# Scores of one head per bank and a fourth bank for row maxima, in two attention stages of one kernel

## The reference, cut to what matters

```python
att = jnp.einsum('bsgmd,btgd->bgmst', q, k) / scale
causal = jnp.triu(jnp.ones((s, s), bool), 1)
att = jnp.where(causal, -jnp.inf, att)
att = jax.nn.softmax(att, axis=-1)
ctx = jnp.einsum('bgmst,btgd->bsgmd', att, v).reshape(b, s, DIM)
```

## Time and profile before

| what | value |
|---|---|
| median of 3 runs | 5195.83 us (5181.3 to 5202.37) |
| profiled execution | 5158.03 us |
| its span | 5156.5 us |
| mean granted clock of TensorE | 0.887 |
| attention B, first to last score | 198.7 to 1006.6 us |
| attention G, first to last score | 2316.2 to 3166.8 us |

### The profile page before, as it was taken

The page is one execution under the profiler, slowest core; times in us unless marked ns, Lnnn a source line. Parts: engine busy times, 40 slices in busy tenths (PEclk is TensorE's granted clock), DMA queues, the critical chain, the costliest instruction groups (busy, mean ns, idle before and its releaser), DMA issues. The chain is left out here.

```text
span 5156.5 us, 83448 instructions
## 1 busy us (share of the span) xinstructions
PE 4120.5 (80%) x25572; PEld 2739.7 (53%) x25572; DVE 3024.9 (59%) x5338; ACT 2489.3 (48%) x4335; POOL 1363.3 (26%) x2120
## 2 busy tenths in 40 slices
PE   4799999753999994659999996576996967699687
PEld 2444444343999992324444442454665755466465
DVE  1788878441444543748878783575563447656454
ACT  1377767612545541217767675233553423355343
POOL 1232323124000005011111111133882003388300
PEclk9699989976999997858979898798998989899898
DMA  7322322123121203361422221334451023444211
GB/s 227 40 33 33 51 35 33 45 101 108 49 88 49 70 31 119 123 115 26 64 43 45 43 45 64 109 120 142 155 156 51 28 57 115 147 148 156 73 37 37
DMA packets 327112, 413.90 MB, mean 80 GB/s; under 512 B 40772, under 2 KB 236225, under 8 KB 323196
## 3 DMA queue, kind: packets, MB, share of 16 engines
q1 hardware_dynamic: 278620, 257.43, 15.8%
q0 software_dynamic: 43552, 148.12, 13.5%
q10 hardware_dynamic: 4608, 4.20, 0.2%
HBM read 252.57 MB, written 156.19 MB: 79 GB/s over the span
## 5 line engine op out<-in xcount | busy, mean ns | idle before, releaser
L600 DVE TENSOR_REDUCE G_mpart<-G_pm 128x1 f32<-128x512 f32 (+3 forms) x1024 | 618.4, 651 | 209.6 <-PE G_pm L489 202.2
L600 DVE TENSOR_REDUCE B_mpart<-B_pm 128x1 f32<-128x512 f32 (+3 forms) x1024 | 618.1, 651 | 157.3 <-PE B_pm L489 149.3
L579 ACT ACTIVATE G_p<-G_psc 128x1024 f32<-128x1024 f32 (+1 forms) x576 | 532.9, 977 | 151.7 <-PE G_psc L526 149.9
L579 ACT ACTIVATE B_p<-B_psc 128x1024 f32<-128x1024 f32 (+1 forms) x576 | 532.2, 977 | 134.6 <-PE B_psc L526 132.8
L489 PE MATMUL G_pm<-G_ks,G_qs 48*128 48x512 f32 (+3 forms) x1664 | 466.3, 425 | 100.3 <-DMA G_ks<-G_one 58.4
L489 PE MATMUL B_pm<-B_ks,B_qs 48*128 48x512 f32 (+3 forms) x1664 | 453.7, 410 | 74.8 <-DMA B_ks<-B_one 42.5
L489 PEld LDWEIGHTS G_pm<-G_ks,G_qs 48*128 48x128 f32 x1664 | 253.0, 212 | 421.3 <-DVE G_mpart L600 210.7
L1786 POOL TENSOR_SCALAR J_pr<-J_pr,J_rc 128x256 f32<-128x256 f32 x512 | 462.8, 916 | 39.9 <-DVE J_rc L1924 37.5
L489 PEld LDWEIGHTS B_pm<-B_ks,B_qs 48*128 48x128 f32 x1664 | 241.8, 200 | 386.2 <-DVE B_mpart L600 218.7
L504 PE MATMUL G_po<-G_p,G_v 128*32 128x512 f32 (+3 forms) x2560 | 326.6, 592 | 0.1
L526 PE MATMUL G_psc<-G_qs,G_ks 50*128 50x512 f32 (+3 forms) x1280 | 307.0, 418 | 9.3 <-issue 6.8
(11 more groups left out here) (303 smaller groups left out, 7895.3 us busy)
## 6 DMA issues: line engine op xcount, KB each, us to landing
J_v<-lve SPq DMA_DIRECT2D x64, 520.0 KB, 3.8
J_k<-lkT SPq DMA_DIRECT2D x64, 512.0 KB, 4.9
lve<-I_v SPq DMA_DIRECT2D x64, 260.0 KB, 2.1
lqT<-I_tT SPq DMA_DIRECT2D x64, 256.0 KB, 2.4
lkT<-I_tT SPq DMA_DIRECT2D x64, 256.0 KB, 2.6
J_q<-lqT SPq DMA_DIRECT2D x64, 256.0 KB, 3.8
ein<-Z_z SPq DMA_DIRECT2D x8, 1228.0 KB
E_xin<-ein POOLq DMA_DIRECT2D x8, 1152.0 KB, 6.2
```

The source lines that it names most:

```text
L579: act.activation(p[:, t % PSLOTS, 2 * pr:2 * pr + 2, span(t)], psc[:, 2 * pr:2 * pr + 2, span(t)], ACT.Exp, scale=SC).then_inc(e_done[pr], 1)
L600: dve.tensor_reduce(mpart[:, heads[0] % 2, a:z, qb, kc], pm[slots[e]][:, 0:len(heads) * w].rearrange("p (h k) -> p h k", k=w), AX, ALU.max ...
```

## The change

There are three edits, and all are inside `attention`. The tensor `psc` of four banks (a pair of heads each for two exponentials) becomes a ring of three banks, one head each, and the freed bank goes to the ring for events, which has four. ACT has an exponential for each head over 512 columns, and one semaphore `e_done` counts them. PE's order in a step becomes S0, W, S1, P, S2, S3 and the remaining P.

```diff
-    RING = 3
+    RING, SBANKS = 4, 3
-        psc = ctx.enter_context(nc.psum_tensor(tag + "psc", [P, GRP, CH], F32))
+        psc = [ctx.enter_context(nc.psum_tensor(f"{tag}psc{i}", [P, CH], F32)) for i in range(SBANKS)]
@@ pool, clear
-                    wait_apart(pool, e_done[pr], i * NS + t + 1, fence)
+                    wait_apart(pool, e_done, i * (NS * GRP) + t * GRP + 2 * pr + 2, fence)
@@ tensor, weigh
-                for pr in range(2):
-                    pe.wait_ge(e_done[pr], i * NS + t + 2)
+                pe.wait_ge(e_done, i * (NS * GRP) + t * GRP + GRP + 1)
@@ tensor, body
-                    for pr in range(2):
-                        pe.wait_ge(e_done[pr], i * NS + t + 1)
+                    def score(h):
+                        if not static(i, 0) or t * GRP + h >= SBANKS:
+                            pe.wait_ge(e_done, i * (NS * GRP) + t * GRP + h + 2 - SBANKS)
                         for kb, off, at in parts:
-                            for h in (2 * pr, 2 * pr + 1):
-                                rows = slice(64 * (h % 2), 64 * (h % 2) + R + 2)
-                                score = pe.matmul(psc[:, h, at:at + CH - off],
+                            rows = slice(64 * (h % 2), 64 * (h % 2) + R + 2)
+                            last = pe.matmul(psc[(t * GRP + h) % SBANKS][:, at:at + CH - off],
...
-                        score.then_inc(s_done, 1)
-                        some(pr, pr + 1)
-                    if t >= 2:
-                        weigh(i, s, t - 2)
-                    elif not static(i, 0):
-                        weigh(i - 1, 1 - s, NS - 2 + t)
-                    some(2, NE)
+                        last.then_inc(s_done, 1)
...
+                    score(0)
+                    weigh_behind()
+                    score(1)
+                    some(0, 1)
+                    score(2)
+                    score(3)
+                    some(1, NE)
@@ scalar, body
-                    for pr in range(2):
-                        act.wait_ge(s_done, (i * NS + t) * 2 + pr + 2)
+                    for h in range(GRP):
+                        act.wait_ge(s_done, i * (NS * GRP) + t * GRP + h + 2)
...
-                        act.activation(p[:, t % PSLOTS, 2 * pr:2 * pr + 2, span(t)],
-                                       psc[:, 2 * pr:2 * pr + 2, span(t)],
-                                       ACT.Exp, scale=SC).then_inc(e_done[pr], 1)
+                        act.activation(p[:, t % PSLOTS, h, span(t)], psc[(t * GRP + h) % SBANKS][:, span(t)],
+                                       ACT.Exp, scale=SC).then_inc(e_done, 1)
```

More of the change, by code:

```diff
@@ L298, in attention @@
         s_done, pv_done = sem(tag + "s_done"), sem(tag + "pv_done")
-        e_done = [sem(f"{tag}e_done{i}") for i in range(2)]
+        e_done = sem(tag + "e_done")
         cleared = sem(tag + "cleared")
@@ L519, in some, with weigh_behind @@
                             event(i + nxt, e, (s + nxt) % 2)
-                    for pr in range(2):
-                        pe.wait_ge(e_done[pr], i * NS + t + 1)
+                    def score(h):
+                        if not static(i, 0) or t * GRP + h >= SBANKS:
+                            pe.wait_ge(e_done, i * (NS * GRP) + t * GRP + h + 2 - SBANKS)
                         for kb, off, at in parts:
-                            for h in (2 * pr, 2 * pr + 1):
-                                rows = slice(64 * (h % 2), 64 * (h % 2) + R + 2)
-                                score = pe.matmul(psc[:, h, at:at + CH - off],
-                                                  ks[s][rows, h // 2 % NA, kb * P:(kb + 1) * P],
-                                                  qs[s][rows, qc, h // 2, off:CH], start=True, stop=True)
-                        score.then_inc(s_done, 1)
-                        some(pr, pr + 1)
-                    if t >= 2:
-                        weigh(i, s, t - 2)
-                    elif not static(i, 0):
-                        weigh(i - 1, 1 - s, NS - 2 + t)
-                    some(2, NE)
+                            rows = slice(64 * (h % 2), 64 * (h % 2) + R + 2)
+                            last = pe.matmul(psc[(t * GRP + h) % SBANKS][:, at:at + CH - off],
+                                             ks[s][rows, h // 2 % NA, kb * P:(kb + 1) * P],
+                                             qs[s][rows, qc, h // 2, off:CH], start=True, stop=True)
+                        last.then_inc(s_done, 1)
+                    def weigh_behind():
+                        if t >= 2:
+                            weigh(i, s, t - 2)
+                        elif not static(i, 0):
+                            weigh(i - 1, 1 - s, NS - 2 + t)
+                    score(0)
[5 more added lines that the diff above has]
+                    some(1, NE)
             pe.wait_ge(c_in, 16 * CONSTS)
```

## The result

The kernel became slower: 5281.85 us (5275.04 to 5295.12, four runs) against 5191.39 us before (5181.3 to 5202.37, four runs beside them), ratio 1.019 [1.016, 1.021]. I had forecast 5235 us with a range to 5315: the sign is right, the loss is more than twice the +39. The profiled execution took 5280.8 us, 123 more than that of before, while the medians differ by 90.

What follows compares the result with a forecast made beforehand. It took a ring of three banks closing over the weighting, PE and DVE waiting for each other, as the bound. Terms -8 + 23 + 14 + 10 = +39 us gave 5197, plus 38 for the runs' median 5235 us; range 5150 to 5315.

Steps and rivals of the forecast that it cites:

- +39: Whole kernel: sum of the forecast's terms, -8 + 23 + 14 + 10 us.
- Regular step, 2.61 for 2.70: Regular attention step: DVE's loop of 2.70 us opens and a loop through ACT of 2.61 us replaces it.
- copy_out, 1.07 of wait: First weighting of a chunk waits for ACT's copy: 1.07 us, 0.65 in 256-column steps, +3.4 us per iteration.
- POOL's zeros, +14 in B: Step 8 of B: the weighting waits 2.7 us for POOL's zeros, six loads; +14 us, bounds 0 and 16.
- An iteration, 98.6 us: One undisturbed iteration of 36 steps: 98.6 us against 99.3 before, 0.7 us less.
- DVE's term: Steps of five events and gathering maxima (24, 25, 33, 34): +2.9 us per iteration, bounds 0 and 5.
- G keeps half: Attention G: gains of steps 5 to 15 go into the load's wait in step 16, so about half is kept.
- The tail, +11.6 each: Last 18 steps of each attention, without events: 2.61 us loop holds, 47.3 us against 35.7, +23 in all.
- The clock, +10 with bounds 0 and 40: B: POOL's new wait may bring the lower clock for four or five steps, 6 to 8 us a stretch.
- Rival 3: Each new wait of 1.07 us and more brings the lower clock for some 16 us, tail too; 5307 us, chance 0.15.
- rival 1: Fourth bank smooths crowded steps, with no POOL or clock cost: -23, or -43 with half the copy_out wait, 5153; chance 0.2.

Runs made afterwards that it cites:

- half_max: The changed kernel with every maximum reading only the first half of its columns; 5252.72 us, ratio 1.012 to the kernel before.
- evict_late: The changed kernel with ACT's evictions moved behind the first exponential of the next step; 5297.03 us, ratio 1.018 to the kernel before.
- Both repairs together: The changed kernel with copy_out behind a step's first exponential and the load's queries issued in step 6 behind the zeros; 5182.99 us, ratio 1.001.
- copy_first: The changed kernel with copy_out behind the first of a step's four exponentials instead of behind all four; 5248.27 us, ratio 1.014.
- before_copy_late2: The kernel before with a finished chunk's copy moved behind both pairs of exponentials of the next step; 5457.11 us, ratio 1.051.
- filler: The changed kernel with four more unread matmuls per step from step 19 of the last iteration on; 5279.66 us, ratio 1.020.
- before_copy_late1: The kernel before with a finished chunk's copy moved behind the first pair of exponentials of the next step; 5272.54 us, ratio 1.017.
- banks_old_order: The changed kernel's banks and one exponential for each head, with PE's order of before; 5970.54 us, ratio 1.151.
- heads_apart: The kernel before with an exponential for each head, four score banks and three event banks, old order; 5186.22 us, ratio 0.998.

## Why the prediction was right or wrong

- **Regular step, 2.61 for 2.70.** Right to 0.01, and the loop named was the one that was there. But only 12 of an iteration's 36 steps last 2.60 to 2.62; before, 18 last 2.70 or 2.71. The sum for 2.70 only adds up distances between rows that follow each other, so that it had to meet 2.70; that DVE's loop set it is borne out by its waits, which fell to a fifth.
- **`copy_out`, 1.07 of wait.** Right (1.06). What I left unpriced is that such a wait can lower the clock: 8 of 41 did.
- **POOL's zeros, +14 in B.** Right in sum: 16.3 us. The six long ones were of 1.7 to 3.4 us, 12.6 in sum, where I had 2.7 each; shorter ones make the rest. In G, where I had put them at nothing, they sum to 8.0 us.
- **An iteration, 98.6 us.** Too low, and this step failed too: a gain of 0.7 us was a loss of 1.8. In G, in an iteration at the full clock and without a wait for the load, the weighting of step 9 stands at 2756.64 and the next iteration's at 2858.64, 102.0 us; 0.9 of it is a wait for POOL's zeros, so that 101.1 answers to my 98.6. The window of it:

```profile
2756.60:2858.60 102.00, 96.31 (x693) 48.09 (x692) 85.04 (x149) 81.97 (x170) 20.16 (x69) 1.00 0.31 50
```

  DVE's term was 0.7 too small (`half_max`), since it sits in eleven steps and not in four; the evictions of step 2 had no term (0.4, `evict_late`). About 1.4 us is spread over steps that I did not take apart. In B's seven iterations and a half this is +18 us.
- **G keeps half.** G's main part fell by 5 us and I had about 3, which is luck. Its iterations were too low in my sum by the same 2.5 us, and this execution made up for it with less low time in the whole main part (from 162 to 96 us); two others of the same main part took 828 and 836 us, 19 and 27 more than before. The load's wait went from 11.0 us to 7.0:

```profile
PE G_pm L489 <- DMA G_v<-vs: 7.0, 3, 3.1
```

- **The tail, +11.6 each.** The step that failed. The loop's 2.61 held for the first steps, and then its matmul terms grew at the granted clock 0.50 to steps of 4.07: 64.1 and 63.6 us where I had 47.3. I had put the clock's part in the tail at nothing. I had trusted this term most, and had priced the tail at the clock of the earlier trace rows, where PE was busy for 94% of the time (33.41 of 35.70 us). Missing: 33 us.
- **The clock, +10 with bounds 0 and 40.** The step that failed in the main part. I priced one stretch for some of POOL's waits at 6 to 8 us. Low time in B's main part rose by 87 us; at 2.61 against 4.07 us for the same step that costs 87 x 1.46 / 4.07 = 31 us. Some 61 us of it, 22 us by the same estimate, stand behind waits of weightings (75 against 14); 23 more came in from the opening and differ so between executions. Both repairs together remove what stands behind the weightings' waits, and such a wait in the old order brings it back. Rival 3 had the mechanism for POOL's waits, and its 5307 was nearer than the forecast; its count was not right, since most waits of 1.06 us brought nothing, and the tails fall without the copy's wait too (`copy_first`). Against it I had set that B before stood at 0.96 among hundreds of short waits; but the one of the earlier trace rows is of 0.5 us, and the new ones are of 1.1 to 3.4.

From +39: +18 (iterations in B), +21 (clock in B), +33 (tails), -2 (G) give +109 against 107 measured in the two attentions. That is the account of one pair of executions, in which before was 33 us under its median; the medians differ by 90. The 21 is an estimate by the steps' lengths at either clock, and the -2 is measured, not explained. In rival 1, the 2.9 us is counted for 13 iterations, while the sum counts seven and half of seven; with 10.5 of them its -23 would be -15.

The Trainium skill (TensorE: Matmul & The Clock Gate, "A second HAM failure mode: psum-queue depth-cycling") says that a kernel which cycles through PSUM banks with short idle pieces pays each time the clock falls and recovers. I had argued against it from the 0.96. The tails agree with it: in `copy_first` the clock falls with no wait above 0.55 us in the 8 us ahead. In the main parts the low stretches stand for the most part behind longer idle times.

## What to carry to other kernels

Price a new wait of TensorE twice: once as the wait, and once as the stretch at the lower clock that may follow. In these kernels it followed 21 of 24 waits of 1.7 us and more and 8 of 41 of 1.06 us, and in `before_copy_late2` it cost more than the waits. A single repair may be too small to see in the total, so look at the stretch it was meant for, and compare with several executions. Work a loop out term by term from the timeline (it came out right to 0.01 us), and then ask whether the idle time that it leaves allows the clock at which its terms were read, above all in a tail with no other work.

## What the runs showed of the hardware that was not expected

- Unread matmuls made a stretch faster: 238 to 302 PE records in B's tail, 64.1 to 51.1 us (`filler`).
- In `before_copy_late1` one wait of 1.38 us between stretches in which PE was busy for 96 and 100% was followed by at least 22 us at the granted clock 0.50, in which PE was busy without a gap. Other waits of the same length in that kernel were not followed so.
- The same instructions in the same order, with three banks for scores and four for events (`banks_old_order`), ran B's main part at a granted clock of 0.61 over 1181 us, and with four and three (`heads_apart`) at 0.93 over 783 us.
- Twice in each attention, in nearly every kernel, PE stands idle for 3 to 4 us with no wait that the profile names (7.4 us in sum in B after the change, 6.8 before), and low stretches of 3 to 48 us follow.
